# Gathering attention rows in steps of 16 slots with halves of 8, and picking the target logits 16 slots at a time

## The chip, the cores and the metric

One NeuronCore of a Trainium2 chip runs one launch of the program. The metric is the device time of a launch in microseconds (us), as a median over runs.

## The reference

The network takes x of shape (4, 128, 32, 32), that is 4 images with 128 channels and 4096 positions in all, and applies two blocks, each a convolution and a token network, with residuals:

```python
x = x + deformable_conv(_ln_c(x), ...)          # block 0: offsets, bilinear samples, 3x3
t = to_tokens(x)
t = t + routed_mlp(_ln_t(t), ...)               # block 0: top half of the tokens
x = x + conv3x3(_ln_c(x), weight)               # block 1
t = t + graph_moe(_ln_t(t), ..., edge_index)    # block 1: the part that matters here
```

The last part routes every token to two of four experts by scores from a graph attention layer:

```python
h = (x_flat @ W_gat).reshape(M, HEADS, NUM_EXPERTS)       # M tokens, 4 heads, 4 features each
a_src = (h * att_src).sum(-1); a_dst = (h * att_dst).sum(-1)
e = leaky_relu(a_src[src] + a_dst[dst], 0.2)              # 524288 edges and the self loops
e_max = segment_max(e, dst); ee = exp(e - e_max[dst])
alpha = ee / (segment_sum(ee, dst)[dst] + 1e-16)
agg = segment_sum(h[src] * alpha[:, :, None], dst) + b_gat
scores = _layernorm(agg, ln_gamma, ln_beta).reshape(M, HEADS, NUM_EXPERTS).mean(1)
topk_s, topk_i = top_k(scores, 2); w = softmax(topk_s)
for ei in range(4):                                       # experts: 128 -> 256 -> 128, exact GELU
    out += g_ei * (gelu(x @ W1[ei] + b1[ei]) @ W2[ei] + b2[ei])
```

Indices beyond the 4096 tokens are clamped or dropped, so only few edges carry a weight of their own; those are the ones that the kernel gathers.

## The kernel before

The program is written by hand, with one instruction stream for each engine (the functions under `nc.Block`: SyncE `sp`, GpSimd `pool`, ScalarE `act`, VectorE `dve`, TensorE `pe`) and semaphores between them. No planner orders anything: each engine runs its stream as it stands in the file. Loops (`Fori`) are loops of the program on the engines.

Earlier stages sort the edges that matter into slots: each of the 128 partitions holds a list of keys (`slot_k`), 16 keys a round, ordered by target. The number of steps that the gather has to make is computed on the chip: VectorE takes the largest number of keys that a partition holds, adds `STEP - 1` and shifts right (L1243, L1244), and GpSimd and VectorE load the result as the bound of their loops (L573, L1457).

The stage that the change touches comes after the third layer norm (`ln3`):

- VectorE decodes the keys (`slot_keys`, L1327): source row `slot_idx`, target column `his`, and `ends`, where the target changes. It makes a table of 4096 rows of 20 numbers (16 features and 4 source logits), which SyncE writes to HBM (`table_d`).
- GpSimd gathers (`gather`, L577). A step has two halves. For each half it waits until VectorE has emptied that half's buffer (`max1_done`), copies the half's indices to `g_idx` (L583), and issues one indirect DMA for each slot (L588); each fetches 128 rows of 20 numbers to one column of `rows_step`, and counts on one of the four semaphores `rows_landed`. VectorE gives two releases ahead, so the first two halves need none.
- VectorE processes (`slot_step`, L1355). For each half of four slots: compare `his` with the lane numbers (L1363), multiply the one-hot result with the target logits of all heads, `bucket_dst` (L1365), and reduce (L1367); the result is the target logit of each slot. Then it waits for the half's rows, copies the features to `feat_s` (L1371, tile `taps_w`), adds the source logits (L1372, tile `kept`) and releases the half (`max1_done`, L1374). The helper `chained` puts a wait behind each step.
- After the last step `slot_scans` (L1379) runs over all 128 slot columns: a maximum scan, differences, then it asks ScalarE for two exponentials (`e_ask`, ScalarE L815) and multiplies features by weights (L1392), and so on.

Beside this, TensorE and ScalarE run the experts, which need only the normed tokens: 8 chunks of 512 tokens times 4 experts, the first chunk written out on TensorE, the other seven in a loop there; ScalarE loops over all eight (`hidden` with GELU at L788, `expert_out`, a copy, at L793). ScalarE's stream has the exponentials of `slot_scans` behind that loop. All TensorE matmuls have the line of the helper `mm`, L1552.

The tiles: `rows_g` holds the landed rows (`rows_step` is a view of its first half), `shared` the one-hot columns and the product grid, `sel` the slot keys and indices.

## Time and profile before

| | |
|---|---|
| median of 3 runs | 1075.08 us (1070.51 to 1075.96) |
| the profiled execution | 1066.97 us, span 1065.2 us |
| mean granted TensorE clock | 0.882 of full speed |
| TensorE busy | 798.7 us, 75% of the span |
| VectorE busy | 666.0 us, 63% |
| ScalarE busy | 364.2 us, 34% |
| GpSimd busy | 173.5 us, 16% |
| indirect DMAs issued by GpSimd | 88, in 11 steps of 8 |
| from the first index copy of the gather to the end of its last DMA instruction | 820.03 to 955.17 us |

Times of the trace are counted from the start of the span. PE is TensorE, PEld its weight loads, DVE VectorE, ACT ScalarE, POOL GpSimd, SP SyncE. "L588" is line 588 of the kernel, and `out<-in` names the tiles. In a time line each row has the start, the duration, the engine, the operation with its tiles and shape, and in brackets the idle time ahead of it and what ended it; "issue" means that nothing in the trace accounts for it, "remote" that the signal was not traced to its sender. A DMA_INDIRECT row of POOL is the time in which GpSimd makes the descriptors, not the transfer.

### The profile page before, as it was taken

The page shows a single profiled execution, that of the slowest core. Times are in us where ns is not written, and L with a number is a line of the kernel's source. Part 1 is how long each engine was busy: PE and PEld are TensorE (multiplying, and loading weights), DVE is VectorE, ACT ScalarE, POOL GpSimd, SP SyncE. Part 2 cuts the span into 40 slices and gives each one's busy share as a digit, 9 for nine tenths or more (in the row PEclk, how much of TensorE's full clock was granted, in tenths as well). Part 3 has the DMA queues.
Part 4 walks back from the last instruction along what each step waited for, and adds up shares of the span by engine and source line. Part 5 has one row for each costly group of instructions (what it writes and reads, how often), then busy time and mean ns, then how long its engine had stood idle before and what let it go on. Part 6 is the DMA issues. An engine that isn't in the chain of part 4 may idle for free.

```text
span 1065.2 us, 14646 instructions
## 1 busy us (share of the span) xinstructions
PE 798.7 (75%) x4525; PEld 497.0 (47%) x4565; DVE 666.0 (63%) x1427; ACT 364.2 (34%) x559; POOL 173.5 (16%) x201
## 2 busy tenths in 40 slices
PE   4359920017998989989988788799859969766768
PEld 1212210016887868878853233344316324223757
DVE  3699778755656656647648776586564533334567
ACT  4421130004544544534452233340021625346350
POOL 5180010000000000000022000100001576760011
PEclk9589965557999999999999899999978989988689
DMA  8000000010000000000000000000010010110001
GB/s 311 0 1 1 1 0 0 2 43 39 2 1 0 0 0 0 0 0 0 0 0 1 0 0 0 2 1 0 2 42 14 6 7 7 7 7 0 3 1 79
DMA packets 11421, 15.50 MB, mean 15 GB/s; under 512 B 5568, under 2 KB 9152, under 8 KB 10992
## 3 DMA queue, kind: packets, MB, share of 16 engines
q1 hardware_dynamic: 8288, 13.87, 3.6%
q0 software_dynamic: 3088, 1.08, 1.5%
q8 instruction: 22, 0.36, 0.1%
q14 instruction: 23, 0.19, 0.1%
HBM read 10.35 MB, written 4.59 MB: 14 GB/s over the span
## 4 chain that ended last, share of the span: by engine, by line
PE 29%; DVE 13%; issue 6%; another core or an unknown queue 3%; ACT 3%; DVEq 1%; POOL 0%; ACTq 0%; DMA 0%; PEld 0%; PEldq 0%; POOLq 0%; SPq 0%
PE banks L1552 25%; DVE kept L1227 2%; PE banks L1904 2%; DVE wide_buf L1187 1%; PE banks L1833 1%; DVE wide_buf L1193 1%; DVE tie L1191 1%; DVE kept L1290 1%; DVE T L865 1%; DVE round_k L1289 1%; PE banks L1585 1%; ACT wide_buf L775 1%; ACT XP L788 0%; DVE shared L1398 0%
## 5 line engine op out<-in xcount | busy, mean ns | idle before, releaser
L1136 DVE TENSOR_TENSOR wide_buf<-banks,small 128x1024 f32<-128x1024 f32 x72 | 88.2, 1224 | 117.8 <-ACT small L725 117.8
L1552 PE MATMUL banks<-wide_buf 128*128 128x256 f32 (+1 forms) x720 | 144.5, 348 | 0.0
L1552 PEld LDWEIGHTS banks<-wide_buf 128*128 128x128 f32 x720 | 122.2, 194 | 12.5
L1552 PE MATMUL banks<-XP 128*128 128x32 bf16 (+1 forms) x1168 | 101.0, 227 | 35.8 <-DVE XP L990 27.4
L1552 PE MATMUL banks<-taps_w,small 128*128 128x128 f32 x618 | 92.3, 296 | 20.4 <-issue 20.4
L723 ACT ACTIVATE small<-banks,neg_x 128x512 f32<-128x512 f32 x72 | 49.5, 687 | 150.6 <-remote 64.7
L1552 PEld LDWEIGHTS banks<-taps_w,small 128*128 128x128 f32 x618 | 85.6, 203 | 31.1 <-issue 21.5
L1552 PEld LDWEIGHTS banks<-XP 128*128 128x128 bf16 (+1 forms) x1168 | 62.0, 109 | 75.0 <-issue 45.7
L588 POOL DMA_INDIRECT rows_g<-table_d,g_idx x88 | 84.9, 965 | 37.6 <-issue 32.9
L1552 PE MATMUL banks<-T,XP 128*128 (+1 forms) x128 | 69.1, 660 | 20.5 <-issue 10.6
L739 ACT COPY wide_buf<-banks 128x512 f32<-128x512 f32 (+1 forms) x87 | 49.6, 570 | 96.5 <-PE banks L1552 95.8
L1552 PE MATMUL banks<-shared,sel 128*128 x180 | 52.3, 386 | 35.5 <-DVEq L1129 26.8
L990 DVE TENSOR_TENSOR XP<-lo_b,XP 128x2048 bf16<-128x2048 bf16 x64 | 77.8, 1215 | 0.0
L1552 PE MATMUL banks<-XP,rows_g 128*32 128x512 f32 x144 | 63.9, 603 | 2.5 <-issue 2.5
L1552 PE MATMUL banks<-XP,taps_w 128*128 x144 | 62.1, 593 | 1.2 <-ACT wide_buf L775 1.2
L622 ACT ACTIVATE shared<-T 128x512 f32<-128x512 f32 x32 | 20.1, 629 | 116.9 <-DVE T L853 116.9
L1552 PE MATMUL banks<-X,mean_w 128*128 128x512 f32 x64 | 35.1, 670 | 30.4 <-DVE X L1322 15.9
L788 ACT ACTIVATE XP<-banks,m_b 128x512 f32<-128x512 f32 x64 | 43.4, 687 | 36.1 <-PE banks L1552 19.2
L1552 PEld LDWEIGHTS banks<-T,XP 128*128 128x128 f32 x128 | 24.8, 206 | 59.0 <-issue 37.0
L725 ACT ACTIVATE small<-small 128x512 f32<-128x512 f32 x72 | 45.4, 631 | 2.3
L1552 PEld LDWEIGHTS banks<-XP,taps_w 128*128 128x128 f32 x144 | 27.1, 189 | 35.6 <-issue 35.6
L547 POOL COPY small<-T 128x1024 f32 x3 | 3.1, 1039 | 248.6 <-PE banks L1552 248.6
(341 smaller groups left out, 1210.8 us busy)
## 6 DMA issues: line engine op xcount, KB each, us to landing
wide_buf<-in_edges SPq DMA_DIRECT2D x2, 1536.0 KB, 14.7
generic_d<-generic SPq DMA_DIRECT2D x1, 2064.0 KB, 7.3
X<-in_x SPq DMA_DIRECT2D x4, 512.0 KB, 4.9
out_x<-X SPq DMA_DIRECT2D x4, 512.0 KB, 2.6
rows_g<-table_d,g_idx POOLq DMA_INDIRECT x88
wide_buf<-in_edges SPq DMA_DIRECT2D x2, 512.0 KB, 9.4
XP<-in_m_w SPq DMA_DIRECT2D x2, 512.0 KB, 4.8
taps_w<-in_w_dcn SPq DMA_DIRECT2D x1, 576.0 KB, 16.7
```

What stands on the lines that cost most here:

```text
L588: pool.indirect_dma_start(rows_step[:, half, k, :], None, table_d, bass.IndirectOffsetOnAxis(ap=g_idx[:, c:c + 1], axis=0)).then_inc(rows_ ...
L622: nc.scalar.activation(squares[:, i % 6, :], T[:, i, :], ACT.Square).then_inc(ln.squared, 1)
L723: nc.scalar.activation(hat_x[:, h, :], ps[2][:, :], ACT.Abs, bias=neg_x[:, :]).then_inc(ax_done, 1)
L725: nc.scalar.activation(hat_x[:, h, :], hat_x[:, h, :], ACT.Relu, bias=1.0, scale=-1.0).then_inc(rx_done, 1)
L739: nc.scalar.copy(out, tiles.rearrange("p (t c) -> p t c", c=P)).then_inc(yt_done, 1)
L775: nc.scalar.activation(routed[:, q * CHUNK:(q + 1) * CHUNK], ps[4 + q % 2][:, :], ACT.Relu, bias=neg_lo[:, :]).then_inc(turned_out, 1)
L788: nc.scalar.activation(mid[:, e % 2, c, :], ps[2 + c][:, :], ACT.Gelu, bias=m_b1[:, e, c:c + 1]).then_inc(mid_done, 1)
L990: return nc.vector.tensor_tensor(out_, digits.rearrange("p (a b) -> p a b", b=2).unsqueeze(2).to_broadcast(grid), lane_pair[:, 0:out_.shap ...
L1136: nc.vector.tensor_tensor(near_w[s % RING], banks[:, 0:2, :], hat_x[:, h:h + 1, :].to_broadcast([P, 2, CHUNK]), ALU.mult).then_inc(w_done, 1)
L1227: last = nc.vector.max(kept2[:, 8 * c:8 * c + 8], parts[:, c, :])
L1552: return nc.tensor.matmul(o, l, r, start=start, stop=stop, **kw)
L1904: last = nc.tensor.transpose(ps[2 + e][:, j * P:(j + 1) * P], y_exp[e][:, i, j * P:(j + 1) * P], ident[:, :])
```

## The change

`STEP` becomes 16, so a half has 8 slots. `rows_step` is now all of `rows_g`, whose second half was not used in this stage. The bound of the loops is computed with a shift by 4. In `slot_step` the compare, the multiply and the reduction are made once for all 16 slots, ahead of the two halves; each half then only waits, files and releases. The four semaphores of landed rows count four DMAs each in place of two. The expert loops are not touched. Between the two files lines after 54 lie one lower, and those after L1371 two.

```diff
--- before.py
+++ after.py
@@ -51,7 +51,8 @@
 HALFR = ROUND // 2
 MAX_BATCHES = -(-ECOLS // BATCH)
 WAYS = P // ROUND
-STEP = 8
+STEP_BITS = 4
+STEP = 1 << STEP_BITS
 HALF_STEP = STEP // 2
 STEPS = P // STEP
 MAX_ROUNDS = ECOLS * P // ROUND
@@ -121,7 +122,7 @@
 
 
         rows_g = sb("rows_g", [P, 2, HALFR, ROW])
-        rows_step = rows_g[:, 0, :, :].rearrange("p (a k) f -> p a k f", a=2)
+        rows_step = rows_g
         vals2 = sb("vals2", [P, 2, HALFR, ROW])
         w_off = rows_g[:, :, :, :].rearrange("p a k f -> p (a k f)")[:, 0:TAPS * 32].rearrange("p (k c) -> p k c", c=32)
         b_off = sb("b_off", [32, 1])
@@ -249,8 +250,8 @@
         decay = f_w1[:, :]
         v_den = f_w2[:, :, :].rearrange("p c d -> p (c d)")
         v_agg = shared[:, 0:HE * P]
-        oh_slots = shared[:, 3200:3200 + HALF_STEP * HIS].rearrange("p (k t) -> p k t", t=HIS)
-        pick_grid = shared[:, 0:HALF_STEP * HEADS * HIS].rearrange("p (k h t) -> p k h t", h=HEADS, t=HIS)
+        oh_slots = shared[:, 3200:3200 + STEP * HIS].rearrange("p (k t) -> p k t", t=HIS)
+        pick_grid = shared[:, 0:STEP * HEADS * HIS].rearrange("p (k h t) -> p k h t", h=HEADS, t=HIS)
         sums_t = small[:, :].rearrange("p (n f) -> p n f", f=SUMS)
         oh_ends = generic[:, 0:P * HIS].rearrange("p (n t) -> p n t", t=HIS)
         node_new = shared[:, 3200:3200 + HIS * SUMS].rearrange("p (t f) -> p t f", f=SUMS)
@@ -586,7 +587,7 @@
                     for k in range(HALF_STEP):
                         c = half * HALF_STEP + k
                         pool.indirect_dma_start(rows_step[:, half, k, :], None, table_d,
-                                                bass.IndirectOffsetOnAxis(ap=g_idx[:, c:c + 1], axis=0)).then_inc(rows_landed[half][k // 2], 16)
+                                                bass.IndirectOffsetOnAxis(ap=g_idx[:, c:c + 1], axis=0)).then_inc(rows_landed[half][k // (HALF_STEP // 2)], 16)
 
             pool.wait_ge(ends_ready, 1)
             with pool.Fori(0, steps) as r:
@@ -1241,7 +1242,7 @@
                 run(nc.vector.tensor_scalar(e_ab, counts_max[:, :], float(ROUND - 1), None, ALU.add))
                 steps_ = num[:, N_STEPS:N_STEPS + 1]
                 run(nc.vector.tensor_scalar(steps_, counts_max[:, 0:1], float(STEP - 1), None, ALU.add))
-                run(nc.vector.tensor_scalar(steps_, steps_, 3, None, ALU.logical_shift_right))
+                run(nc.vector.tensor_scalar(steps_, steps_, STEP_BITS, None, ALU.logical_shift_right))
                 run(nc.vector.tensor_scalar(e_ab, e_ab, 4, None, ALU.logical_shift_right))
                 run(nc.vector.memset(counts[:, 1:2], 0.0))
                 full = dve.value_load(num[0:1, N_EB:N_EB + 1], min_val=0, max_val=(1 << 17) // ROUND)
@@ -1322,7 +1323,7 @@
                     nc.vector.tensor_tensor(X[:, i, :], X[:, i, :], bank_of(i), ALU.add).then_inc(res3, 1)
             norm(ln3, res3, 2)
 
-            SLOT_KEYS, SLOT_STEP = 11, 2 * (3 + 1)
+            SLOT_KEYS, SLOT_STEP = 11, 3 + 2
 
             def slot_keys(R):
 
@@ -1357,16 +1358,17 @@
                 g = R * STEPS + r
                 step, n = chained(m1_chain, g * SLOT_STEP, True)
 
+                cols = bass.ds(r * STEP, STEP)
+                grid = [P, STEP, HEADS, HIS]
+                step(nc.vector.tensor_tensor(oh_slots, his[:, cols].unsqueeze(2).to_broadcast([P, STEP, HIS]),
+                                             lane[:, 0:HIS].unsqueeze(1).to_broadcast([P, STEP, HIS]), ALU.is_equal))
+                step(nc.vector.tensor_tensor(pick_grid, oh_slots.unsqueeze(2).to_broadcast(grid),
+                                             bucket_dst[:, :, :].unsqueeze(1).to_broadcast(grid), ALU.mult))
+                step(nc.vector.tensor_reduce(z_by_head[:, :, cols].rearrange("p h k -> p k h"), pick_grid, AX_X, ALU.add))
                 for half in range(2):
                     cols = bass.ds(r * STEP + half * HALF_STEP, HALF_STEP)
-                    grid = [P, HALF_STEP, HEADS, HIS]
-                    step(nc.vector.tensor_tensor(oh_slots, his[:, cols].unsqueeze(2).to_broadcast([P, HALF_STEP, HIS]),
-                                                 lane[:, 0:HIS].unsqueeze(1).to_broadcast([P, HALF_STEP, HIS]), ALU.is_equal))
-                    step(nc.vector.tensor_tensor(pick_grid, oh_slots.unsqueeze(2).to_broadcast(grid),
-                                                 bucket_dst[:, :, :].unsqueeze(1).to_broadcast(grid), ALU.mult))
-                    step(nc.vector.tensor_reduce(z_by_head[:, :, cols].rearrange("p h k -> p k h"), pick_grid, AX_X, ALU.add))
                     for landed in rows_landed[half]:
-                        dve.wait_ge(landed, g * (16 * 2) + 16 * 2)
+                        dve.wait_ge(landed, g * (8 * HALF_STEP) + 8 * HALF_STEP)
                         dve.sem_inc(passed, 1)
                     nc.vector.tensor_copy(feat_s[:, :, cols], rows_step[:, half, :, 0:HE].rearrange("p k f -> p f k"))
                     step(nc.vector.tensor_tensor(z_by_head[:, :, cols], z_by_head[:, :, cols],
```

In VectorE's stream, at the body of the slot loop (`slot_step`; tile `kept` is the slots' logits, `taps_w` the features), the order was:

```order
L1363 TENSOR_TENSOR shared<-sel,lane 128x128
L1365 TENSOR_TENSOR shared<-shared,bucket_dst 128x512 [waits m1_chain]
L1367 TENSOR_REDUCE kept<-shared 128x4x4
L1371 REGISTER_ALU [waits rows1_in,rows1_b]
L1371 COPY taps_w<-rows_g 128x16x4
L1372 TENSOR_TENSOR kept<-kept,rows_g 128x4x4
L1363 ISA [waits m1_chain]
L1363 TENSOR_TENSOR shared<-sel,lane 128x128
L1365 TENSOR_TENSOR shared<-shared,bucket_dst 128x512 [waits m1_chain]
L1367 TENSOR_REDUCE kept<-shared 128x4x4
L1371 REGISTER_ALU [waits m1_chain,rows2_in,rows2_b]
L1371 COPY taps_w<-rows_g 128x16x4
```

and is now:

```order
L1363 TENSOR_TENSOR shared<-sel,lane 128x512
L1365 TENSOR_TENSOR shared<-shared,bucket_dst 128x2048 [waits m1_chain]
L1367 TENSOR_REDUCE kept<-shared 128x16x4
L1371 ISA [waits m1_chain]
L1373 REGISTER_ALU [waits rows1_in,rows1_b]
L1373 COPY taps_w<-rows_g 128x16x8
L1374 TENSOR_TENSOR kept<-kept,rows_g 128x4x8
L1373 ISA [waits m1_chain,rows2_in,rows2_b]
L1373 COPY taps_w<-rows_g 128x16x8
L1374 TENSOR_TENSOR kept<-kept,rows_g 128x4x8
```

The pick of the second half has moved ahead of the wait for the first half's rows, and is part of one operation of four times the elements of each former one.

In GpSimd's stream, one half of a step (tile `g_idx` holds the indices) was

```order
L583 ISA [waits max1_done]
L583 COPY g_idx<-sel 128x4
L588 DMA rows_g<-table_d,g_idx 128x20 [waits idx1_ready]
L588 DMA rows_g<-table_d,g_idx 128x20 x3
```

and is now

```order
L584 ISA [waits max1_done]
L584 COPY g_idx<-sel 128x8
L589 DMA rows_g<-table_d,g_idx 128x20 [waits idx1_ready]
L589 DMA rows_g<-table_d,g_idx 128x20 x7
```

with one wait for a release in front of eight DMAs where there was one in front of four.

## Rows read from the trace of the kernel before

**Rows 1.** Time line of DVE: first slot step, two later ones, the last.

```profile
835.03 0.29 DVE L1363 TENSOR_TENSOR shared<-sel,lane 128x128 f32<-128x128 f32 x1 [1.61 <-issue]
...
843.06 0.69 DVE L1367 TENSOR_REDUCE kept<-shared 128x512 f32 x1 [0.23 <-issue]
...
851.49 0.29 DVE L1371 COPY taps_w<-rows_g 128x64 f32 x1 [3.02 <-DMA rows_g<-table_d,g_idx]
851.62 0.18 DVE L1372 TENSOR_TENSOR kept<-kept,rows_g 128x16 f32 x1
852.42 0.29 DVE L1363 TENSOR_TENSOR shared<-sel,lane 128x128 f32<-128x128 f32 x1 [0.62 <-DVE kept L1372]
852.86 0.69 DVE L1365 TENSOR_TENSOR shared<-shared,bucket_dst 128x512 f32<-128x512 f32 x1
853.78 0.69 DVE L1367 TENSOR_REDUCE kept<-shared 128x512 f32 x1 [0.23 <-DVE shared L1365]
...
957.82 0.21 DVE L1371 COPY taps_w<-rows_g 128x64 f32 x1 [3.07 <-DMA rows_g<-table_d,g_idx]
957.95 0.18 DVE L1372 TENSOR_TENSOR kept<-kept,rows_g 128x16 f32 x1
958.53 0.69 DVE L1382 SCALAR_TENSOR_TENSOR kept<-kept 128x512 f32<-128x512 f32 x1 [0.40 <-DVE kept L1372]
```

**Rows 2.** Time line of ACT: starts of passes of the expert loop, and its end.

```profile
833.08 1.28 ACT L788 ACT_TABLE_LOAD   x1
...
848.13 1.28 ACT L788 ACT_TABLE_LOAD   x1
...
862.86 0.58 ACT L793 COPY wide_buf<-banks 128x512 f32 x1 [3.79 <-PE banks L1552]
...
874.99 1.28 ACT L788 ACT_TABLE_LOAD   x1
...
957.57 1.28 ACT L788 ACT_TABLE_LOAD   x1
...
972.71 1.28 ACT L824 ACT_TABLE_LOAD   x1
```

**Rows 3.** Waits from 815 us on: us in total, times, longest.

```profile
DVE shared L1392 <- ACT f_w L815: 11.8, 1, 11.8
POOL g_idx L583 <- DVEq L1374: 6.6, 1, 6.6
```

**Rows 4.** Windows: busy us of each engine, granted clock, DMA share, GB/s.

```profile
core 0: us, PE busy (x) PEld busy (x) DVE busy (x) ACT busy (x) POOL busy (x), PEclk, DMA share, GB/s
860.00:880.00 20.00, 10.75 (x16) 3.95 (x15) 5.28 (x14) 5.79 (x8) 13.78 (x19) 0.73 0.10 7
900.00:920.00 20.00, 17.09 (x38) 6.61 (x37) 7.41 (x17) 9.12 (x13) 14.27 (x18) 1.00 0.10 7
```

**Rows 5.** Time line of POOL: index copies and DMA issues of the gather.

```profile
820.03 0.19 POOL L583 COPY g_idx<-sel 128x4 int32 x1 [73.87 <-DMA table_d<-shared]
...
830.81 0.94 POOL L588 DMA_INDIRECT rows_g<-table_d,g_idx  x1 [0.30 <-issue]
838.35 0.26 POOL L583 COPY g_idx<-sel 128x4 int32 x1 [6.60 <-DVEq L1374]
...
843.17 0.94 POOL L588 DMA_INDIRECT rows_g<-table_d,g_idx  x1 [0.30 <-issue]
...
849.83 0.19 POOL L583 COPY g_idx<-sel 128x4 int32 x1
850.81 0.97 POOL L588 DMA_INDIRECT rows_g<-table_d,g_idx  x1 [0.79 <-issue]
...
853.33 1.04 POOL L588 DMA_INDIRECT rows_g<-table_d,g_idx  x1 [0.30 <-issue]
...
855.62 0.19 POOL L583 COPY g_idx<-sel 128x4 int32 x1
...
954.23 0.94 POOL L588 DMA_INDIRECT rows_g<-table_d,g_idx  x1 [0.30 <-issue]
```

**Rows 6.** Groups by form: mean ns of one, for 2048 elements on DVE.

```profile
L1222 DVE SCALAR_TENSOR_TENSOR wide_buf<-wide_buf 128x2048 f32<-128x2048 f32 x6 | 13.8, 2292 | 8.7 <-ACT wide_buf L775 8.7
```

**Rows 7.** The gather's line: duration ns min/median/max, first and last start us.

```profile
L588 POOL DMA_INDIRECT rows_g<-table_d,g_idx x88: 940/944/1196, 821.1 to 954.2; - x88
```

## The prediction

> **What bounds the kernel now.** I read the time line of the stretch from 815 us on, engine by engine, and then the list of waits, because the change touches only what runs there. Two strings of work run side by side in it and meet at 972 to 974 us. The first is the gather of attention rows: GpSimd issues 88 indirect DMAs, VectorE picks target logits and files the rows that landed. The second is the expert MLP, in loops on TensorE and ScalarE. VectorE's next work, the scans, needs both: the slots from the gather, and two exponentials that ScalarE makes only when its expert loop is over.
>
> What to see in the rows: the gather ends at 957.95 + 0.18 and the scans start at 958.53 [rows 1]. The expert loop on ScalarE makes seven passes between its table loads of 833.08 and 972.71 [rows 2]. VectorE then stands for 11.8 us in front of L1392 until ScalarE delivers [rows 3]. So **the experts set the end, and the gather has 11.8 us to spare**. After 974 everything is in series and is not touched.
>
> The expert loop is not at its own pace. Its first pass takes 848.13 - 833.08 = 15.05 us, the next 874.99 - 848.13 = 26.86 us [rows 2]; seven passes take 139.63 us where seven at 15.05 would take 105.4, so 34.2 us are lost. In a slow pass ScalarE stands before operations whose inputs have long been there: 3.79 us at 862.86 [rows 2]. TensorE follows ScalarE, and its granted clock is 0.73 in such a stretch against 1.00 in a good one [rows 4], a mean over its two levels of 2.4 and 1.2 GHz. I find no cause of the holes in the trace, and that is what is least sure below.
>
> **The change part by part, against the profiled execution** (span 1065.2 us, 1066.97 with what lies around it; the median of the runs is 1075.08, 8.1 us above, and I carry differences over to it).
>
> *Number of steps.* 88 DMAs in steps of 8 are 11 steps, so the fullest partition has 81 to 88 slots. In steps of 16 that is 6 steps, 12 halves of 8, 96 DMAs: 8 more than before, for slots past the end.
>
> *GpSimd.* A half of four runs from the index copy at 849.83 to the one at 855.62, 5.79 us, of which 0.10 is a held DMA; so 5.69 us [rows 5]. DMAs follow each other every (853.33 - 850.81) / 2 = 1.26 us. A half of eight is 5.69 + 4 x 1.26 = 10.7 us: one index copy and one wait fewer for eight DMAs. Twelve halves are 128.4 us; the first one starts 0.3 us slower than the rest. From 820.03 they would end at 948.7, if nothing held them. Before, 22 halves of 5.69 are 125.2 us, and the last DMA ends at 954.23 + 0.94 = 955.2 [rows 5]: the other 10 us are the opening wait of 6.6 us [rows 3], 0.3 for the first half and about 3 of small holds and waits.
>
> *The opening wait.* GpSimd issued two halves (8 DMAs) and stood from 830.81 + 0.94 to 838.35, because VectorE begins its first step at 835.03 only [rows 1, 5]. Now two halves are 16 DMAs and last until about 842, while VectorE is through with the pick and the first half at about 835.0 + 5.8 + 0.6 = 841.4 us. The wait goes, to within 0.5 us. That is the gain of 6.6 us.
>
> *VectorE's pick.* Before, per four slots: 0.29 + 0.69 + 0.69 us and gaps [rows 1], four times for 16 slots. Now once, ahead of both halves, as the order of VectorE's instructions shows: the compare on 512 elements 0.69, the multiply and the reduction on 2048 elements. The nearest row for 2048 is L1222, 2.29 us [rows 6]; the bounds are 0.69 (no longer than for 512) and 4 x 0.69 = 2.8. I take 2.29 for both. With gaps 5.8 us a step, once in 21.4 us: no load on VectorE, and all of it beside DMAs in flight. What is behind the wait on VectorE: before half 1's rows nothing but half 0's filing, 0.5 us, so GpSimd always gets its release early.
>
> *GpSimd held by VectorE.* This is the cost that the change adds. The DMA at 853.33 starts while VectorE's multiply L1365 (852.86 to 853.55) runs and takes 1.04 us; the longest takes 1.196, where the median is 0.944 [rows 1, 5, 7]. 1.04 = 853.55 + 0.82 - 853.33: the held DMA ends 0.82 us after the multiply. A DMA that starts within the reduction L1367 (843.06 to 843.75), the one at 843.17, takes 0.94, so the reduction holds nothing [rows 1, 5]. The new multiply is 2.29 us, longer than the 1.26 between two starts, so it meets one every time. Where it meets it, counted from the end of GpSimd's half, which is the index copy at 849.83: the rows are filed at 851.49, 1.66 later; the next compare starts 0.93 after that, at 852.42; the compare is now 0.69 long and followed by 0.15, so the multiply starts at 3.43 and ends at 5.72. GpSimd's third DMA starts at 853.33 - 849.83 = 3.50 [rows 1, 5]. If it falls inside, it is held by 5.72 + 0.82 - 0.94 - 3.50 = 2.1 us; if it slips by, the fourth, at 4.76, is held by 0.8. The two differ by less than 0.1 us in where the multiply starts, so I take the mean, 1.5, for five steps, and 1.0 in the first, where the multiply runs from 835.9 to 838.2: 8.5 us. The bounds are 11.5 (2.1 each time) and 0 (the hold doesn't scale and is lost).
>
> The Trainium skill (SBUF — State Buffer, Who interferes with whom) says that a VectorE operation with two SBUF inputs contends with GpSimd instructions that read SBUF, and infers in the same place that tensor_tensor nevertheless does not stall DMA, since descriptor generation needs the write interface. The 1.04 us row speaks against the inference. By it the gather would end 5.5 us earlier than before.
>
> *The other moves.* The index copies halve (22 to 12), the filing operations halve in number and double in width, all under the DMAs. The last half lands 2.65 us after its last DMA as before (955.17 to 957.82), and filing it is some 0.1 us longer.
>
> *Sum for the gather.* 948.7 + 8.5 + 1 (what else the former 3 us held) = 958.2, against 955.2: **3 us later**, between 5.5 us earlier (no hold) and 6 later. All of it is inside the 11.8 us that VectorE waits for ScalarE anyway. *Sum for the kernel:* 0 us, as the experts' instructions don't change. With the cover gone it would be the gather's own -5.5 to +6.
>
> **The rivals.**
>
> *A. Forecast: the experts still end last and lose as much in holes as before.* For it: 11.8 us of cover against a shift of at most 6. Against it: nobody knows what makes the holes. 1075.1 us, with 4 us either way for the holes' own spread (the three runs of before lie within 5.5 us).
>
> *B. Faster: the holes come with the gather's traffic and shrink.* For it: there are no holes once the gather is over; the pass from 957.57 on [rows 2] takes 15.14 us. VectorE now issues some 7 instructions for 16 slots in place of 20, and GpSimd 96 operations and 12 copies. One slow pass less is 26.86 - 15.05 = 11.8 us: 1063. Against it: DMAs per us stay at 0.7 and there are 8 more; the pass from 833.08 to 848.13 has the same DMAs beside it and no hole [rows 2, 5].
>
> *C. Slower: the gather's end becomes the bound.* GpSimd is held by the long multiply, and by more than I take: if the 2.29 us reduction held it too, each step would add another 1.4 us or so, and the gather would end 6 + 6 x 1.4 = 14 us later; it decides from 11.8 us on. With the profile's cover that costs only 2 us. In the timed runs, where the experts may lose less, the whole shift would show: 6 to 14 us, so 1081 to 1089. For it: the held DMA; against it: the row of the reduction. The same side has the holes growing with 96 in place of 88 DMAs: 34.2 x 8/88 = 3 us.
>
> *D. The gather bounds the timed runs and is not held:* 4.5 to 6.6 us faster, about 1069.6. It needs both the skill's inference and experts without holes.
>
> *E. The change does less than it says:* more than 6 steps. 88 DMAs exclude it.
>
> **How the numbers follow.** A 0.55, B 0.14, C 0.22 (with the growing holes), D 0.09, E 0. A measurement of this kernel can tell about 0.5%, 5.4 us, from no change. Of A some 0.50 lies within it and the rest on either side in equal parts; B is faster; of C 0.17 is over and 0.05 within; D is half in, half out. Faster 0.20, same 0.59, slower 0.21. The likeliest time is A's, 1075. The range takes in B's one slow pass less and most of C: 1064 to 1086; A's own is 1071 to 1079.
>
> **What the changed profile would show.** 96 DMA_INDIRECT in 12 halves; no wait of 6.6 us before the third index copy; one DMA of 1.8 to 3 us in each step (if none is above 1.3 us, the hold was wrong); the multiply and the reduction at 2.3 us, six of each; VectorE's scans starting at about 961.5; its wait for the exponential before L1392 down from 11.8 to about 9 us and still there; ScalarE's seven passes at about 140 us. The prediction fails if that last figure moves by over 5 us, or if the wait before the exponential's product is gone.

## The result, and the profile after

The kernel after takes 1109.7 us (median of 4, 1101.01 to 1120.86), the kernel before 1072.8 beside it (median of 4, 1069.41 to 1075.96): a ratio of 1.032, 95% interval 1.020 to 1.043. The forecast of no change, with a range to 1086, was wrong. The profiled execution is the slowest of the four, 1120.86 us with a span of 1119.1, some 20 us above the fastest, so the loss that is read from it below is the upper end, while the ratio leaves it out.

The gather did what was forecast. VectorE, start, duration, operation, idle time ahead and its cause, against [rows 1]:

```profile
838.50 2.31 DVE L1365 TENSOR_TENSOR shared<-shared,bucket_dst 128x2048 f32<-128x2048 f32 x1
841.05 2.29 DVE L1367 TENSOR_REDUCE kept<-shared 128x2048 f32 x1 [0.24 <-issue]
...
858.75 0.30 DVE L1373 COPY taps_w<-rows_g 128x128 f32 x1 [5.01 <-DMA rows_g<-table_d,g_idx]
...
869.47 0.29 DVE L1373 COPY taps_w<-rows_g 128x128 f32 x1 [10.32 <-DMA rows_g<-table_d,g_idx]
...
961.56 0.69 DVE L1384 SCALAR_TENSOR_TENSOR kept<-kept 128x512 f32<-128x512 f32 x1 [0.40 <-DVE kept L1374]
```

GpSimd, against [rows 5]:

```profile
822.69 0.19 POOL L584 COPY g_idx<-sel 128x8 int32 x1 [73.68 <-DMA table_d<-shared]
...
839.74 1.89 POOL L589 DMA_INDIRECT rows_g<-table_d,g_idx  x1 [0.30 <-issue]
841.94 0.95 POOL L589 DMA_INDIRECT rows_g<-table_d,g_idx  x1 [0.30 <-issue]
845.37 0.21 POOL L584 COPY g_idx<-sel 128x8 int32 x1
...
957.17 0.95 POOL L589 DMA_INDIRECT rows_g<-table_d,g_idx  x1 [0.30 <-issue]
```

And the gather's line by its source (count, duration ns min/median/max, first and last start), against [rows 7]:

```profile
L589 POOL DMA_INDIRECT rows_g<-table_d,g_idx x96: 941/947/2135, 823.8 to 957.2; - x96
```

96 DMAs, no opening wait, the pick at 2.3 us an operation, one DMA per step that takes 1.9 to 2.1 us in place of 0.94, the last one over at 958.12 (forecast 958.2), the scans at 961.56 (forecast 961.5). What went wrong is ScalarE's expert loop, against [rows 2]; each table load begins a pass:

```profile
814.15 1.28 ACT L789 ACT_TABLE_LOAD   x1 [12.00 <-PEq L1881]
...
843.22 1.28 ACT L789 ACT_TABLE_LOAD   x1
...
867.10 1.28 ACT L789 ACT_TABLE_LOAD   x1
...
910.54 0.59 ACT L794 COPY wide_buf<-banks 128x512 f32 x1 [7.22 <-remote]
919.64 0.59 ACT L794 COPY wide_buf<-banks 128x512 f32 x1 [8.52 <-remote]
920.24 1.28 ACT L789 ACT_TABLE_LOAD   x1
...
965.51 1.28 ACT L789 ACT_TABLE_LOAD   x1
...
980.56 1.28 ACT L789 ACT_TABLE_LOAD   x1
...
1025.80 1.28 ACT L825 ACT_TABLE_LOAD   x1
```

The second pass takes 23.9 us, the third 53.1, the fourth 45.3, and from 965.51 on, when the gather is over, each takes 15.05. Seven passes take 182.6 us against 139.6 before: 43.0 us more; the first pass, before them, is 7.5 us longer, and it starts 2.7 us later. Their sum, 53.2 us, is nearly all of the 53.9 between the two spans. The waits from 815 us on (total, times, longest), against [rows 3]:

```profile
DVE taps_w L1373 <- DMA rows_g<-table_d,g_idx: 81.2, 11, 10.5
DVE shared L1394 <- ACT f_w L816: 61.8, 1, 61.8
```

and the windows, against [rows 4] (busy us of each engine, granted clock, DMA share, GB/s):

```profile
900.00:920.00 20.00, 6.75 (x8) 2.50 (x8) 5.03 (x7) 2.10 (x4) 14.76 (x17) 0.59 0.12 7
980.00:1000.00 20.00, 17.90 (x42) 7.53 (x41) 0.00 (x0) 13.13 (x19) 0.00 (x0) 1.00 0.00 0
```

TensorE makes 8 matmuls in 20 us where it makes 42 after the gather. The low clock (0.59, between the levels 1.2 and 2.4 GHz) follows the idle stretches. Look at one hole from TensorE's side:

```profile
907.01 3.18 PE L1554 MATMUL banks<-T,XP 128*128 x4
923.86 2.08 PE L1554 MATMUL banks<-T,XP 128*128 x2 [13.66 <-ACT XP L789]
```

TensorE is through at 910.19 and waits 13.66 us for ScalarE, whose next GELU is at 923.12; ScalarE meanwhile waits for TensorE's signals, and its copies come at 910.54 and 919.64. Neither engine is working; what is late is the signals from TensorE to ScalarE. The trace has all 64 GELUs of the loop and all the matmuls that they wait for, so each can be set beside its own. The GELU of 923.12 belongs to the matmul that ends at 908.93, the one of 926.65 to the one that ends at 910.19: 14.2 and 16.4 us later, with ScalarE free before. (The profile models the ends of matmuls, but their starts are recorded, and the last of this stretch is at 909.57.) Of the 64, 26 came over 0.6 us late while ScalarE stood idle for them; in the kernel before 18, the latest by 6.8 us.

### The profile page after: what moved, and what is told of

It is laid out like the page before. It is cut to its first block, busy times and chain, and to the rows that moved or that the text cites. A ratio compares the mean times of both kernels' runs of the same rounds, so it can differ in the third digit from the quotient of the medians.

```text
span 1119.1 us, 14329 instructions
## 1 busy us (share of the span) xinstructions
PE 818.4 (73%) x4525; PEld 503.5 (45%) x4565; DVE 658.4 (59%) x1359; ACT 364.7 (33%) x559; POOL 184.1 (16%) x199
## 4 chain that ended last, share of the span: by engine, by line
PE 28%; DVE 12%; issue 7%; another core or an unknown queue 5%; ACT 3%; DVEq 1%; ACTq 0%; POOL 0%; DMA 0%; PEld 0%; PEldq 0%; POOLq 0%; SPq 0%
PE banks L1554 25%; DVE kept L1228 2%; PE banks L1906 2%; DVE wide_buf L1188 1%; PE banks L1835 1%; ACT XP L789 1%; DVE wide_buf L1194 1%; DVE tie L1192 1%; DVE kept L1291 1%; DVE T L866 1%; DVE round_k L1290 1%; PE banks L1587 1%; ACT wide_buf L776 1%; DVE shared L1400 0%
## 5 line engine op out<-in xcount | busy, mean ns | idle before, releaser
L1554 PE MATMUL banks<-XP 128*128 128x32 bf16 (+1 forms) x1168 | 108.6, 234 | 44.8 <-DVE XP L991 27.4
L1554 PE MATMUL banks<-T,XP 128*128 (+1 forms) x128 | 76.5, 719 | 47.1 <-ACT XP L789 39.1
L1554 PEld LDWEIGHTS banks<-XP 128*128 128x128 bf16 (+1 forms) x1168 | 64.3, 111 | 89.6 <-issue 58.2
L589 POOL DMA_INDIRECT rows_g<-table_d,g_idx x96 | 97.8, 1019 | 35.2 <-issue 34.3
L1373 DVE COPY taps_w<-rows_g 128x128 f32 x12 | 3.7, 305 | 81.7 <-DMA rows_g<-table_d,g_idx 81.2
## 6 DMA issues: line engine op xcount, KB each, us to landing
taps_w<-in_w_dcn SPq DMA_DIRECT2D x1, 576.0 KB, 16.4
```

The source lines that it names most:

```text
L589: pool.indirect_dma_start(rows_step[:, half, k, :], None, table_d, bass.IndirectOffsetOnAxis(ap=g_idx[:, c:c + 1], axis=0)).then_inc(rows_ ...
L1554: return nc.tensor.matmul(o, l, r, start=start, stop=stop, **kw)
```

## The experiments

Two figures are read from each profile. **Spacing** is the mean time between the starts of two indirect DMAs of the gather, (last - first) / (count - 1): 1.530 us before, 1.404 after. **Lost** is how much longer the eight passes take than the 127 us that they need without holes (e3, e7, e13, e14: 126.8 to 127.7; with the loops of TensorE and ScalarE written out 114.4, e15 and e16; e2, with one of them written out, lies between, so its loss is given by bounds). Each is from one execution, while the times are medians, so they show which kernels have holes and roughly how large. The spacing counts the opening wait where there is one: without its longest gap it is 1.448 us before, 1.445 in e9, 1.492 in e7, and 1.393 after. Four chips took part; "beside it" is the median of the kernel before beside that run on its chip. The chip of the first two rows is not on record, and the kernel after was run again on chip D alone (e17), so across chips the ratios to the kernel before are compared.

| run | median us | beside it | chip | spacing us | lost us |
|---|---|---|---|---|---|
| before, as profiled | 1075.1 | | | 1.530 | 34 |
| after, as profiled | 1109.7 | 1072.8 | | 1.404 | 85 |
| e1 PE and ACT experts written out | 1060.2 | 1068.7 | A | 1.413 | 55 |
| e2 ACT experts written out | 1075.0 | 1068.7 | A | 1.422 | 34 to 46 |
| e3 no indirect DMAs | 1034.5 | 1068.7 | A | none | 0 |
| e4 GpSimd and VectorE steps written out | 1063.8 | 1068.7 | A | 1.437 | 18 |
| e5 VectorE steps written out | 1062.5 | 1072.6 | B | 1.436 | 27 |
| e6 GpSimd steps written out | 1094.5 | 1072.6 | B | 1.423 | 52 |
| e7 steps of 8, batched pick | 1060.1 | 1072.6 | B | 1.587 | 1 |
| e8 steps of 16, pick by half | 1097.1 | 1072.6 | B | 1.432 | 62 |
| e9 before, VectorE steps written out | 1056.0 | 1069.0 | A | 1.521 | 18 |
| e10 e5 and SyncE waits | 1064.3 | 1069.0 | A | 1.436 | 30 |
| e11 all four loops written out | 1060.5 | 1069.0 | A | 1.448 | 6 |
| e12 gather without waits by half | 1132.2 | 1069.0 | A | 1.303 | 99 |
| e13 after, DMAs spaced | 1116.9 | 1054.4 | C | 2.025 | 0 |
| e14 e12, DMAs spaced | 1106.0 | 1054.4 | C | 2.015 | 0 |
| e15 e12, experts written out | 1037.8 | 1054.4 | C | 1.262 | 0 |
| e16 e15, DMAs spaced | 1089.1 | 1054.4 | C | 1.868 | 0 |
| e17 after, unchanged | 1073.6 | 1059.1 | D | 1.428 | 27 |
| e18 after, every second DMA spaced | 1088.9 | 1059.1 | D | 1.730 | 0 |

Where the expectations name a theory P or R, it is this. Theory P: long waits of VectorE against a register's value, while indirect DMAs run, hold up other engines' signals. (How a waiting engine reads its semaphore, which e5's expectation supposes, no run shows.) Theory R, which came later: the holes come from how closely GpSimd's indirect DMAs follow one another.

### e1 and e2: the expert loops written out

```diff
-            with act.Fori(0, CHUNKS) as i:
+            for i in range(CHUNKS):
...
-            with pe.Fori(1, CHUNKS) as i:
+            for i in range(1, CHUNKS):
```

e2 has ScalarE's half of it alone.

> The changed kernel with both expert loops (TensorE and ScalarE) written out. Theory A (the holes belong to the loops: waits against a register's value, with the register arithmetic ahead of them, become slow while the gather runs): the passes of the experts take 15 us each, the loop ends near 945 us, the gather at about 958 us sets the end, and the time falls by 60 us and more from 1109.7, to about 1050. Theory B (the gather's traffic delays every signal from TensorE to ScalarE, however it is waited for): the holes stay, the experts end near 1026 and the time stays near 1105.

> The changed kernel with ScalarE's expert loop alone written out; TensorE keeps its loop. If the slow side is ScalarE's register waits: as fast as with both written out, about 1050. If the slow side is TensorE (its signals go out late): no change, about 1105. Both: between.

e1: 1060.23 us, ratio 0.992 (0.989 to 0.995) to before, where the kernel after has 1.032, so theory A came closer. Its profiled execution took 1080.21 us and loses 55 us in holes; the other eight took 1057.4 to 1062.2, and how much they lost can't be read. e2, one run: 1075.04 us, between its two cases, experts over at 980.00. The loops' form matters, but holes are there without it (e11 below still loses 6 us with every loop written out).

### e3: the gather without its DMAs

```diff
-                        pool.indirect_dma_start(rows_step[:, half, k, :], None, table_d,
-                                                bass.IndirectOffsetOnAxis(ap=g_idx[:, c:c + 1], axis=0)).then_inc(rows_landed[half][k // (HALF_STEP // 2)], 16)
+                        nc.gpsimd.memset(small[:, 0:600], 0.0).then_inc(stand_in, 1)
+                        pool.wait_ge(stand_in, g * STEP + c + 1)
+                        nc.gpsimd.memset(rows_step[:, half, k, :], 0.0).then_inc(rows_landed[half][k // (HALF_STEP // 2)], 16)
```

The attention rows are left out; GpSimd clears memory in their place, 0.95 us for each on average, so that it is through at 914 us.

> The changed kernel with no indirect DMA: GpSimd writes zeros to the rows with a memset and counts them itself, in about the same rhythm, so the attention rows are left out of the computation. Theory B (traffic and completions of the DMAs): no hole is left, passes of 15 us, time 1050. Theory A with GpSimd's or VectorE's waits as the disturber: holes of the same size, 1100.

ScalarE's passes in it:

```profile
834.83 1.28 ACT L792 ACT_TABLE_LOAD   x1
...
849.88 1.28 ACT L792 ACT_TABLE_LOAD   x1
...
940.26 1.28 ACT L828 ACT_TABLE_LOAD   x1
```

Seven passes of 15.05 us each, 1034.46 us. VectorE waited 36.5 us for GpSimd, by the same register-valued waits. No GELU comes over 0.04 us late for its matmul, in the five passes beside GpSimd's work or after. It is one execution, but the effect is large: the holes need the indirect DMAs, and the expert loops by themselves make none.

### e4, e5 and e6: who waits against a register

```diff
-            with dve.Fori(0, steps) as r:
+            for r in range(6):
                 slot_step(0, r)
```

That is e5; e6 is the same edit on GpSimd's loop, e4 both.

> The changed kernel with the slot loops of GpSimd and VectorE written out as six steps, so that these two wait for constants; the expert loops stay loops. If VectorE's long waits against a register (10 us at a time now, 3 us before) are what slows the others: no hole is left and the time is about 1050. If it is the DMAs, or the experts' own register waits beside them: no change, 1100 to 1120.

> The changed kernel with VectorE's slot loop alone written out as six steps (its waits for the rows are against constants), GpSimd's stays a loop. Theory P (what delays TensorE's signals to ScalarE beside the DMAs is a long wait of VectorE against a register's value, which reads the semaphore again and again): like both written out, near 1065 us, passes of 15 to 20 us. Theory Q (it is GpSimd's loop): no change, 1100 to 1120.

> The changed kernel with GpSimd's slot loop alone written out; VectorE's stays a loop. Theory P: no change, 1100 to 1120. Theory Q: near 1065.

e4, one run: 1063.78 us, nearer to its 1050 than to its 1100, the gather the bound, 18 us lost. e5: ratio to before 0.993 (0.988 to 0.998), 27 us lost; e6: 1.020 (1.005 to 1.035), 52 us lost. On the same chip, e5 is 32 us faster than e6, and its interval lies clear of the kernel after's (1.020 to 1.043); e6's overlaps with that, so nothing is shown for GpSimd's loop. It looked as if theory P held.

### e7 and e8: the two parts of the change apart

e7 keeps the batched pick and goes back to steps of 8 (`STEP_BITS = 3`, and the old view for `rows_step`). e8 keeps steps of 16 and picks per half of 8, by moving the three operations back under `for half in range(2)`.

> The changed kernel with steps of 8 again (halves of 4, 88 DMAs), but the pick made once for 8 slots: the part of the change that batches the pick, alone. VectorE then waits about 8 times 3 to 5 us. Theory P with the single wait's length deciding: near the kernel before, 1065 to 1080, a little above it. If the batched pick itself (its long multiply, which holds GpSimd) is the cause: near 1110.

> The changed kernel with steps of 16 and halves of 8, but the pick made for each half of 8: the part of the change that lengthens the steps, alone. VectorE's single waits are about 7 us, all alike, in place of 5 and 10. Theory P: holes as large as in the changed kernel or nearly, 1085 to 1110. If the batched pick is the cause: near 1068.

e7: ratio 0.988 (0.977 to 0.998), faster than its expectation; the seven passes are all 15.05 us, and the gather bounds. e8: 1.022 (1.012 to 1.033), 62 us lost, as theory P had it. **It is the long step that costs, not the batched pick.** In e7's GpSimd line

```profile
892.58 1.73 POOL L589 DMA_INDIRECT rows_g<-table_d,g_idx  x1 [0.30 <-issue]
894.62 0.94 POOL L589 DMA_INDIRECT rows_g<-table_d,g_idx  x1 [0.30 <-issue]
895.56 0.20 POOL L584 COPY g_idx<-sel 128x4 int32 x1
896.55 0.96 POOL L589 DMA_INDIRECT rows_g<-table_d,g_idx  x1 [0.79 <-issue]
...
904.75 1.73 POOL L589 DMA_INDIRECT rows_g<-table_d,g_idx  x1 [0.30 <-issue]
```

eight DMAs take 904.75 - 892.58 = 12.2 us: a held one, and two index copies with their gaps. In the kernel before two halves without a wait take 11.4 to 11.9, and in the kernel after 16 take 867.77 - 845.37 = 22.4, so 11.2 for eight. e7 has VectorE's loop and register waits like the kernel before (77.9 us of them, 45.3 there) and no holes, where that one has 34 us. Theory P does not explain this.

### e9 to e12: theory P against its consequences

e9 is e5's edit on the kernel before (11 steps), e11 joins e1 and e4, and e10 adds to e5 a loop of SyncE:

```diff
+            with sp.Fori(0, steps) as r:
+                for half in range(2):
+                    for landed in rows_landed[half]:
+                        sp.wait_ge(landed, r * (8 * HALF_STEP) + 8 * HALF_STEP)
```

e12 rebuilds the gather: every slot has its own place in `rows_all`, so nobody releases buffers.

```diff
-                    pool.wait_ge(max1_done, g * 2 + half + 1)
-                    nc.gpsimd.tensor_copy(g_idx[:, cols], slot_idx[:, bass.ds(r * STEP + half * HALF_STEP, HALF_STEP)]).then_inc(idx1_ready, 1)
+                pool.indirect_dma_start(rows_all[:, k, :], None, table_d,
+                                        bass.IndirectOffsetOnAxis(ap=slot_idx[:, k:k + 1], axis=0)).then_inc(four_landed[k % 4], 16)
...
+                dve.wait_ge(rows_known, R + 1)
+                step(nc.vector.tensor_tensor(z_by_head, z_by_head, rows_all[:, :, HE:ROW].rearrange("p k h -> p h k"), ALU.add))
+                step(nc.vector.tensor_copy(feat_s[:, :, :], rows_all[:, :, 0:HE].rearrange("p k f -> p f k")))
```

> The kernel before, with VectorE's loop over the steps written out as its 11 steps, so that its waits for rows are against constants; nothing of the work is left out. Theory P (waits of VectorE against a register's value, while indirect DMAs run, hold up the signals of other engines): the seven later passes of the experts' loop take 105.4 to 120 us (139.6 in the kernel before, 105.4 without holes), the experts end by 950 us, the gather's end (955 us) becomes the bound, and the time is 1052 to 1062 us. Rival (only waits longer than those of a step of 8 do harm, and the kernel before loses its 34.2 us to something else): 1068 to 1076 us, seven passes at 135 to 145 us.

> The kernel after with VectorE's loop written out (1062.5 us so far) and one thing added: SyncE, which has nothing to do there, waits in a loop against register values for the same landed rows. If a register-valued wait of any engine holds up the others, the holes come back: seven passes at 160 to 190 us (127.3 with VectorE's loop written out) and 1085 to 1120 us. If it has to be VectorE's wait, or if not the wait but VectorE's loop did it, 1060 to 1070 us and seven passes at 120 to 135 us.

> The kernel after with every loop of this stage written out: GpSimd's and VectorE's six steps, TensorE's and ScalarE's experts; no wait of the stage is against a register. Theory P: no holes at all, the eight passes end at about 940 us, the gather's end (964 us) bounds, 1058 to 1063 us. If the remaining 22 us of holes with constant waits have another cause (the long waits themselves, or the DMAs), the experts end at 955 to 985 us and the time is 1058 to 1070 us.

> A rebuilt gather: 11 steps of 8 slots, picked 8 at a time; GpSimd issues every DMA from the slot's own index column into a buffer that holds the rows of all 128 slots, so that it copies no indices and waits for nobody, waits once at the end for all rows, and signals VectorE, which adds the source logits and copies the features for all slots at once. VectorE waits for rows once, against a constant. Theory P: no holes, seven passes at 105.4 us, the experts end at 940 us, the gather at 812 + 88 x 1.245 = 922 us; scans after 928 us; the experts bound: 1034 to 1042 us. If the DMAs by themselves make the holes: experts end at 960 to 980 us and 1050 to 1065 us.

e9's time came out within its range for P, with a ratio of 0.988 (0.981 to 0.995), but its seven passes took 123.4 us, above it. e10: no effect of SyncE's waits, 30 us lost where e5 lost 27. e11: 6 us lost, the experts over at 941.6 us, ratio 0.992 (0.989 to 0.996). **e12 broke theory P**: VectorE waits once, against a constant, and the kernel is the slowest of all, 1132.15 us, outside both of its ranges, ratio 1.059 (1.051 to 1.067). VectorE itself is hit there:

```profile
841.45 1.22 DVE L1369 TENSOR_TENSOR shared<-shared,bucket_dst 128x1024 f32<-128x1024 f32 x1
844.55 1.22 DVE L1371 TENSOR_REDUCE kept<-shared 128x1024 f32 x1 [1.88 <-issue]
851.56 0.43 DVE L1367 TENSOR_TENSOR shared<-sel,lane 128x256 f32<-128x256 f32 x1 [5.78 <-issue]
853.71 1.22 DVE L1369 TENSOR_TENSOR shared<-shared,bucket_dst 128x1024 f32<-128x1024 f32 x1 [1.72 <-issue]
```

5.78 us go by ahead of a compare whose inputs are there and that waits for VectorE's own reduction alone (the longest such gap is 6.5 us). Here it is not the signal that is late: the trace records the reduction's at 845.79, as it ends. What is slow is VectorE's own control instructions, which wait, count and branch: of the five before the compare four take 0.70 to 0.71 us, where most take 0.02 to 0.06. Of 85 recorded during e12's gather 50 take 0.7, of 339 in the kernel before 27, and none in the kernel after, e13 to e18 or e7. So beside the DMAs two things go wrong, and the kernel after shows the late signals alone. Its ScalarE passes are

```profile
858.57 1.28 ACT L793 ACT_TABLE_LOAD   x1
...
944.76 1.28 ACT L793 ACT_TABLE_LOAD   x1
...
962.45 1.28 ACT L793 ACT_TABLE_LOAD   x1
...
977.50 1.28 ACT L793 ACT_TABLE_LOAD   x1
```

86.2 us for one pass beside the gather, and 15.05 from 962.45 on (the last DMA starts at 933.65). What sets e12 apart from the runs before it is that GpSimd never pauses: 88 DMAs, 1.303 us apart.

A rival is code loading. The Trainium skill (Runtime: NRT & Kernel Launch, Instruction fetch mechanics) says that a taken branch out of the two loaded pages stalls until its page has come. By that rule, loops that jump back out of those pages would lose time to such loads. The DMA view of the kernel after from 840 to 950 us has one queue:

```profile
q0 software_dynamic: 2464, 0.79, 12.1%
issues: line engine op xcount, KB each, median us to landing
rows_g<-table_d,g_idx POOLq DMA_INDIRECT x78
```

No packet of an instruction queue moves there, while the page of the whole kernel has two such queues. So the holes of that stretch are not code loading. Nor are the DMA engines full: their share is 12.1%.

### e13 to e16: the DMAs spaced

```diff
                     for k in range(HALF_STEP):
                         c = half * HALF_STEP + k
+                        nc.gpsimd.memset(small[:, 0:100], 0.0).then_inc(spaced, 1)
+                        pool.wait_ge(spaced, g * STEP + c + 1)
```

That is e13; e14 and e16 have the like in e12's and e15's gather, with 150 columns and with one, and e15 is e12 with e1's edit.

> The kernel after, VectorE's loop and its waits against register values as they are, and one thing added: before each indirect DMA GpSimd clears 100 columns of an unused region and waits for itself, some 0.27 us, so that the DMAs start at least 1.5 us apart instead of 1.25 us. Theory R (new, from the runs so far: what makes the holes is how close GpSimd's indirect DMAs follow one another; per 8 DMAs 10.0 us gave holes of 74 us in the seven passes, 11.3 us 77 us, 11.6 us 12 to 34 us, 12.2 us none): the holes go though VectorE waits longer than ever, seven passes at 105 to 112 us, the experts end at 945 us; the gather ends at 975 to 990 us and bounds, 1070 to 1085 us. Theory P (VectorE's long waits against register values): the holes stay, the gather being longer they grow, seven passes over 175 us, 1105 to 1130 us.

> The rebuilt gather without waits by halves (1132 us, seven passes 179 us), with the same kind of spacing: 150 columns cleared before each DMA, starts 1.55 us apart instead of 1.25 us. Theory R: no holes or nearly none, seven passes at 105 to 115 us, the experts end at 940 to 950 us, the last rows are there at about 960 us, 1050 to 1062 us. If the spacing does nothing: 1130 to 1150 us.

> The rebuilt gather without waits by halves and without spacing, TensorE's and ScalarE's expert loops written out (which took 30 to 50 us from the kernel after, and took away the last holes of the kernel with constant waits). If the loops' register instructions are what suffers, the eight passes take 128 to 150 us and the time is 1040 to 1065 us; if it is every signal of TensorE and VectorE whatever the form, 1110 to 1135 us as with the loops.

> Both: experts written out, and a spacing of one column (starts 1.45 to 1.5 us apart). Theory R with the written-out loops' greater tolerance: no holes, the experts end at 940 us, the last rows are there at about 950 us, scans from 955 us: 1047 to 1055 us, the fastest kernel so far. Holes of over 10 us would speak against it.

All holes are gone, with VectorE's register waits up to 15.7 us long in e13. The spacing cost more than meant (1.87 to 2.03 us between DMAs for 1.45 to 1.55), so the gather bounds and the times are high: of e13, e14 and e16 the predicted times failed and the predicted passes held. e15 lost nothing, in neither of the expected ranges: 1037.82 us, faster than the better one. But the kernel before took 1054.4 us on this chip, not 1069, and the kernel after was not run on it, so the chip may have made no holes anyway, and these four runs alone show nothing of the spacing.

### e17 and e18: the control

e17 is the kernel after. e18 spaces every second DMA of it:

```diff
+                        if c % 2:
+                            nc.gpsimd.memset(small[:, 0:1], 0.0).then_inc(spaced, 1)
+                            pool.wait_ge(spaced, g * (STEP // 2) + c // 2 + 1)
```

> The kernel after, unchanged, as the control of the runs with spaced DMAs. The kernel before took 1054.4 us on the chip of those runs and 1069 to 1073 us on two others, so the holes may belong to the chip and not to the spacing. Where the kernel before takes about 1054 us beside this run: if the kernel after takes 1055 to 1065 us, that chip makes no holes and the spaced runs say nothing; if it takes 1090 us or more, the spacing did it. Where the kernel before takes 1069 us or more: 1100 to 1120 us, as before.

> The kernel after with GpSimd's wait for itself before every second indirect DMA alone, so that the starts are about 1.6 us apart on average; VectorE's register waits stay. The gather ends at 990 us. Theory R (the spacing decides): no holes, seven passes at 105 to 112 us, 1085 to 1095 us, on any chip. Theory P (VectorE's register waits) or the chip: where the kernel before takes 1069 us or more, seven passes at 150 us or more and 1100 to 1130 us.

Three passes of ScalarE in e17:

```profile
867.96 1.28 ACT L789 ACT_TABLE_LOAD   x1
...
890.79 1.28 ACT L789 ACT_TABLE_LOAD   x1
...
908.80 1.28 ACT L789 ACT_TABLE_LOAD   x1
...
931.06 1.28 ACT L789 ACT_TABLE_LOAD   x1
```

e18's first and last, with seven passes in 105.5 us:

```profile
833.81 1.28 ACT L794 ACT_TABLE_LOAD   x1
...
939.27 1.28 ACT L830 ACT_TABLE_LOAD   x1
```

On one chip, VectorE's loop and waits the same: 27 us lost at a spacing of 1.428 us, none at 1.730. The single profiled executions carry this, and e17's other run took 1085.89 us, so its profiled one, 1061.21, was the mild one of the two. 12 of e17's GELUs came over 0.6 us late for their matmuls, the latest by 8.9 us; of e18's none over 0.04. Spacing the DMAs by a wait of GpSimd for itself takes the holes away. It does not pay in this form (1088.86 us, ratio 1.027, 1.014 to 1.040), since the gather then ends at 987 us. e17 falls between the two cases of its expectation: there are holes on this chip, but the change costs less there: 1061 and 1086 us beside 1055 to 1066.

## Why the prediction was wrong

**The gather's end was right in part by luck.** 958.2 forecast, 958.12 measured, but the gather began at 822.69 where the sum starts at 820.03. It took 135.4 us, not 138.2: 2.7 us less, and began 2.7 us later, which the forecast did not have. What was too large is mostly the term of the holds, 8.5 us. Where it meets the DMA, the hold ends 0.82 us after the multiply as in [rows 5]: 838.50 + 2.31 + 0.82 = 841.63 = 839.74 + 1.89. But 1.89 us is the whole DMA, so the hold is 0.95, near the 0.8 of the DMA that comes one later and not the 1.5 of the mean: the DMA at 838.49 had slipped by 0.01 us ahead of the multiply. All holds of the gather together are some 6.5 us. e17, the same kernel again, shows the other case, a DMA that starts just inside the multiply:

```profile
892.85 2.29 DVE L1365 TENSOR_TENSOR shared<-shared,bucket_dst 128x2048 f32<-128x2048 f32 x1
...
892.90 3.06 POOL L589 DMA_INDIRECT rows_g<-table_d,g_idx  x1 [0.30 <-issue]
```

3.06 us, so a hold of 2.1, as worked out. The reduction held nothing (the DMA at 841.94 lies in it and takes 0.95). The Trainium skill's inference that tensor_tensor does not stall DMA (SBUF — State Buffer, Who interferes with whom) is contradicted by these rows. In the chances, the parts that are named add up to 0.21 for faster and 0.20 for slower, not the other way round; nothing hangs on it.

**The step that failed** is "Sum for the kernel: 0 us, as the experts' instructions don't change". Their instructions did not change; what they stand beside did. The prediction had the right rival in two places and put it away both times:
- Under B it says "DMAs per us stay at 0.7". They were 88 in 133.1 us before, 0.66 per us, and are 96 in 133.4, 0.72. The 6.6 us wait that was booked as a pure gain was a pause between DMAs, and makes up over half of this difference; with the longest gap left out, the spacing goes only from 1.448 to 1.393 us.
- Also under B, the pass from 833.08 to 848.13 was said to have "the same DMAs beside it and no hole". GpSimd stood still from 831.75 to 838.35 in it [rows 5]. It was the pass with the pause, and spoke for B's mechanism.
- C's "34.2 x 8/88 = 3 us" for growing holes is the term that was mis-sized: 43.0 us in the seven passes and 7.5 in the first of the profiled execution. It scaled with the number of DMAs, 9% more, and the losses more than doubled, from 34 to 85 us. (C's other part, a gather that ends 14 us later, did not come: the scans started at 961.56.)

For a pass to be good, the pause does not have to be in it. In the kernel before the pass from 893.39 to 908.44 has no hole either, with DMAs all along beside it, and GpSimd had stood for 1.19 us shortly before:

```profile
883.31 0.95 POOL L588 DMA_INDIRECT rows_g<-table_d,g_idx  x1 [0.30 <-issue]
885.45 0.18 POOL L583 COPY g_idx<-sel 128x4 int32 x1 [1.19 <-remote]
...
893.39 1.28 ACT L788 ACT_TABLE_LOAD   x1
...
908.44 1.28 ACT L788 ACT_TABLE_LOAD   x1
```

ScalarE's waits of over 1.4 us stop at 886 and come back at 916. In e8 GpSimd stands for 3.29 us until 857.85, and they stop at 861 and come back at 896. So at much the same spacing holes are there or not, and what went before counts; the mean spacing alone can't tell it.

**What is shown.** The time is lost in signals from TensorE that reach ScalarE late. The holes need indirect DMAs (e3, one execution). Steps of 16 in place of 8 make the kernel slower where the pick is made for 8 slots in both (e8 against e7, on one chip, intervals apart). VectorE's register waits are not needed for the holes (e12), and with them there need be none (e7, e18). With VectorE's slot loop written out the kernel is faster (e5 against e6, on one chip).

**What is argued.** That the spacing of the DMAs decides rests on one pair of executions on one chip, 27 us lost in e17 and none in e18, and on e7, which keeps its distance by held DMAs and index copies, without e18's memsets and waits. The pauses in the kernel before and in e8 fit it. The times of this pair do not show it, since e18's longer gather sets its end.

**What stays open.** Of the runs with the expert loops as loops, spacing orders the extremes: 0 to 1 us lost at 1.59 us and above, 99 us at 1.30. It does not order the middle: between 1.40 and 1.45 us 18 to 85 us are lost (6 with every loop written out), and the same kernel lost 85 us in one execution and 27 in another on chip D. e15 lost nothing at 1.262 us, the closest of all, and no run tells whether by its written-out experts or by its chip. By what way GpSimd's indirect DMAs delay TensorE's signals was not found. Every run compared here was recorded by the profiler, so nothing shows whether an unrecorded execution has the holes; that the recording takes part in them is a rival that no run excludes.

**Better versions.** e15, at 1037.8 us, has a ratio of 0.984 (0.981 to 0.988, two runs) to the kernel before on chip C and is the fastest here that does all the work; it was not run on chips A and B. Of those run there, e9, before with VectorE's steps written out, took 1056.0 us in all four runs to within 0.7 (ratio 0.988), but it fixes the number of steps at 11, which other inputs may not fit. e7 keeps that number computed on the chip and took 1060.1 (ratio 0.988, 0.977 to 0.998, two runs).

## What to carry to other kernels

A wait that costs an engine nothing may be what spaces its DMAs: before taking it away, see which other engines' loops run beside that stretch, and whether their good stretches are the ones with a pause in them or just before. When a loop loses time for which the trace has no cause, do not carry the loss over unchanged to a kernel whose neighbours change. And measure the kernel before beside the new one, on more than one chip, before a margin of a few per cent is believed.

## What was unexpected of the hardware

- Beside back-to-back indirect DMAs of GpSimd, signals from TensorE to ScalarE came up to 16.4 us late in the kernel after and up to 24.9 in e12, and VectorE's control instructions took 0.70 us each in e12, up to 6.5 us in front of an operation, while the DMA engines were 12% busy. ScalarE's signals to TensorE came at once (a GELU ends at 903.32, TensorE starts at 903.44).
- After a pause of GpSimd of 1.19 us at 885.45 the kernel before ran some 25 us without a hole, at the spacing of the stretches with holes.
- A GpSimd wait for its own memset of one column put the starts of two DMAs 1.87 us apart (e16) where they are 1.25 us apart without it.
- The kernel before took 1054.4 us (median of 7) on one chip and 1072.6 (median of 9) on another.
